# Attention and experts on one core: chunk order, selection matmuls, experts under the last chunk, and a maximum pass that masks in its own instruction

## The reference, cut to what matters

```python
x = x + xattn(layernorm(x), ctx, mask)      # x: 2048 x 256, ctx: 1601 x 256
x = x + ffn(layernorm(x))

def xattn(query, key, mask):                # 16 heads of 16
    scores = (query @ Wq.T) @ (key @ Wk.T).T / 4       # per head
    scores = where(mask == 0 or key index > query index, -inf, scores)
    context = nan_to_num(softmax(scores)) @ (key @ Wv.T)
    return sigmoid(query @ Wg.T + bg) * context @ Wo.T

def ffn(x):                                 # 8 experts, hidden 128, top 2
    scale = softmax(x @ gate_w), all but the two largest set to 0
    xs = scale[e] * x
    return sum over e of (silu(xs @ w1[e]) * (xs @ w3[e])) @ w2[e]
```

## Time and profile before

| what | us |
|---|---|
| median of 3 timed runs | 730.34 (726.5 to 733.89) |
| the profiled execution, own time | 721.41 |
| its span, first to last instruction | 719.7 |
| PE busy | 655.9 (91%) |
| DVE busy | 500.9 (70%) |
| ACT busy | 387.5 (54%) |
| POOL busy | 87.0 (12%) |
| mean granted TensorE clock, share of full speed | 0.925 |

### The profile page before, as it was taken

The page is one execution under the profiler, slowest core; times in us unless marked ns, Lnnn a source line. Parts: engine busy times, 40 slices in busy tenths (PEclk is TensorE's granted clock), DMA queues, the critical chain, the costliest instruction groups (busy, mean ns, idle before and its releaser), DMA issues.

```text
span 719.7 us, 12305 instructions
## 1 busy us (share of the span) xinstructions
PE 655.9 (91%) x4564; PEld 400.3 (56%) x4564; DVE 500.9 (70%) x1043; ACT 387.5 (54%) x778; POOL 87.0 (12%) x167
## 2 busy tenths in 40 slices
PE   5538999969999999999999999999977899999996
PEld 2415756645564554563545455454422587888885
DVE  3112958947868997867898998979630387767764
ACT  1112166545737676555777776657899543332331
POOL 4011233201302011201010102001100000000000
PEclk9767579969988999987999999989999999999999
DMA  9489950710440100750000050000000510616000
GB/s 296 99 144 149 152 64 3 128 22 2 98 51 3 20 3 31 117 178 2 2 3 1 2 118 3 1 1 4 1 2 1 93 27 2 146 25 123 1 30 30
DMA packets 30037, 39.11 MB, mean 54 GB/s; under 512 B 5272, under 2 KB 15896, under 8 KB 29977
## 3 DMA queue, kind: packets, MB, share of 16 engines
q1 hardware_dynamic: 25398, 35.56, 25.7%
q10 hardware_dynamic: 2530, 2.50, 1.1%
q0 software_dynamic: 2048, 0.27, 0.3%
HBM read 27.94 MB, written 9.64 MB: 52 GB/s over the span
## 4 chain that ended last, share of the span: by engine, by line
PE 71%; issue 9%; DMA 9%; DVE 6%; ACT 3%; SPq 1%; POOL 1%; DVEq 0%; ACTq 0%; POOLq 0%
PE bank L1288 15%; PE bank L1268 13%; PE bank L1241 12%; PE bank L1174 8%; DMA k_parts<-stage 4%; PE bank L1349 4%; PE bank L1350 4%; PE bank L1351 4%; DVE pmax L1031 3%; PE bank L1245 3%; DMA q_parts<-stage 2%; PE bank L1367 2%; PE bank L1369 2%; PE bank L1368 2%; DMA qaug<-m_row 2%
## 5 line engine op out<-in xcount | busy, mean ns | idle before, releaser
L1031 DVE TENSOR_REDUCE pmax<-bank 128x1 f32<-128x512 f32 (+4 forms) x640 | 328.4, 575 | 54.8 <-PE bank L1241 36.5
L899 ACT ACTIVATE probs<-bank 128x512 f32<-128x512 f32 (+4 forms) x592 | 281.5, 551 | 128.3 <-PE bank L1268 78.7
L1241 PE MATMUL bank<-kaug,qaug 49*128 49x512 f32 (+4 forms) x640 | 208.3, 441 | 1.6 <-ACT rest L839 1.0
L1268 PE MATMUL bank<-qaug,kaug 51*128 51x512 f32 (+4 forms) x592 | 189.9, 444 | 9.5 <-DMA qaug<-m_row 6.4
L1288 PE MATMUL bank<-probs,vaug 128*32 128x512 f32 (+4 forms) x1184 | 146.3, 580 | 8.8 <-ACT probs L899 8.8
L1268 PEld LDWEIGHTS bank<-qaug,kaug 51*128 51x128 f32 (+1 forms) x592 | 88.1, 190 | 110.7 <-ACT probs L899 58.1
L1241 PEld LDWEIGHTS bank<-kaug,qaug 49*128 49x128 f32 x640 | 106.8, 202 | 34.6 <-DVE pmax L1031 14.7
L1245 PE MATMUL bank<-tri_b,eye_b 64*128 64x128 bf16 (+1 forms) x416 | 60.4, 248 | 0.0
L1288 PEld LDWEIGHTS bank<-probs,vaug 128*32 128x32 f32 (+1 forms) x1184 | 25.6, 111 | 52.2 <-ACT probs L899 31.8
L1349 PE MATMUL bank<-x_hi,w_hi 128*128 128x512 f32 x128 | 51.4, 402 | 0.0
L1350 PE MATMUL bank<-x_lo,w_hi 128*128 128x512 f32 x128 | 50.8, 397 | 0.0
(11 more groups left out here) (104 smaller groups left out, 675.4 us busy)
## 6 DMA issues: line engine op xcount, KB each, us to landing
qaug<-s_dram SPq DMA_DIRECT2D x4, 2048.0 KB, 15.5
qaug<-q_parts SPq DMA_DIRECT2D x24, 256.0 KB, 8.8
kaug<-k_parts SPq DMA_DIRECT2D x18, 256.0 KB, 8.8
q_parts<-stage SPq DMA_DIRECT2D x8, 512.0 KB, 8.2
k_parts<-stage SPq DMA_DIRECT2D x6, 512.0 KB, 13.8
x_sb<-in_x ACTq DMA_DIRECT2D x4, 512.0 KB, 12.0
w_sb<-in_w SPq DMA_DIRECT2D x4, 512.0 KB, 5.4
out<-x_sb SPq DMA_DIRECT2D x4, 512.0 KB, 6.2
```

The lines of the kernel that those rows point to most:

```text
L899: act.activation(probs[0:rows, u % NSLOT, h, off:CH], bank_of(e)[0:rows, off:CH], ACT.Exp, scale=DK ** -0.5).then_inc(act_read, 1)
L1031: dve.tensor_reduce(pmax[:, n % 2, qt, h, slot:slot + 1], bank[:, 0:w], AX_X, ALU.max).then_inc(dve_read, 1)
L1241: last = pe.matmul(bank[:, 0:w], qaug[b:b + ROW_MAX, c % 2, hp, P * qt:P * (qt + 1)], kaug[b:b + ROW_MAX, hp, k0:k0 + w], start=True, stop ...
L1268: last = pe.matmul(bank[0:r, off:CH], kaug[b:b + ROWS, hp, P * j:P * j + r], qaug[b:b + ROWS, c % 2, hp, off:CH], start=True, stop=not dia ...
```

## The change

- Chunks are taken in the order 1, 2, 3, 0 (`ORDER`; `POS` is a chunk's place). Chunk 1 needs keys 0 and 1, so `KEYS_OF` loads both first. Inputs are loaded in another order, some on other queues.
- The first half of the dimensions (`m` = 0: heads 0 to 7) of keys 0 and 1 and of chunk 1's queries doesn't go through DRAM: `sel`, matmuls with a selection matrix of ones, put the parts of two heads at a time where they belong, with mask rows and rows of ones, and ScalarE and VectorE by turns copy the bank to `kaug0`, `kaug1`, `qaug`. The other half takes the trip as before.
- `kaug` is split: `kaug0` for keys 0 to 511, which is all chunk 0 needs, `kaug1` for the rest. `w_hi`, `x_hi` and an expert buffer lie over `kaug1` only. So `ws`, `xs` and the experts of chunk 1 may begin once all scores of chunk 3 are made, beside the attention of chunk 0.
- The maximum pass makes no mask matmuls. VectorE reduces a diagonal piece with `tensor_tensor_reduce`: adds a bf16 tile `causal`, takes the maximum, and writes the sum back to PSUM. `max_pieces` cuts at 512 first and then evenly, as many pieces as before.
- `y` is made turned: six matmuls of 512 columns into two banks, copied by ScalarE (`ycopy`), turned back by TensorE (`yT`), added by VectorE, and written in halves of a chunk. `y` runs two experts behind `a` and `b`, not one.
- GpSimd takes from VectorE the norm (except the first), the parts of weights (`ws`), x's low part, the product `h` and its low part. Scales are loaded per expert. The planner's costs and preferences are new.

The diff, cut to its core:

```diff
+ORDER = (1, 2, 3, 0)
+POS = {c: p for p, c in enumerate(ORDER)}
-Y_BANKS = (0, 1, 2, 7)
+Y_BANKS = (5, 6)
+KEYS_OF = ((0, 1), (2,), (3,), ())
...
+    if p == 0:
+        select = {(w, k): [("sel", w, k, pair) for pair in range(4)] for w, k in (("k", 0), ("k", 1), ("q", c))}
+        return [*norm, ("kq", "k", 0, 0), ("kq", "k", 0, 1), *select["k", 0], *turn, *select["k", 1], ("kq", "q", 0, c),
+                ("kq", "k", 1, 0), *select["q", c], ("kq", "k", 1, 1), ("kload", p), ("kq", "q", 1, c), ("qload", p), *values, *gate]
...
         if kind == "xs":
-            return [("xT1", e[1], 1)] + ([("b", e[1] - 2, E - 1)] if e[1] >= 2 else []) + ([("prologue_end",)] if not e[1] else [])
+            p = POS[e[1]]
+            n = G * (NC - 1) - 1
+            late = [("prologue_end",), ("mred", n)] + all_st(n) if not p else []
+            return [("logits", e[1])] + ([("b", ORDER[p - 2], E - 1)] if p >= 2 else []) + late
...
+        if name == "maxima" and e[1] >= G * (NC - 1):
+            return first_at[e] + 5000
         if name in ("scores", "maxima") and consumer(e) and e[0] != "mT":
-            return free[consumer(e)] - pe_time(e) - DRAIN
+            return free[consumer(e)] - pe_time(e) - DRAIN - (AHEAD if name == "scores" else 0)
...
+            kaug1 = sb("kaug1", [P, HP, KP - CH], F32R, attention)
         w_hi = sb("w_hi", [P, E, 3, D], F32R)
+        x_hi = sb("x_hi", [P, 2, KD, CH], F32R)
+        u_even = sb("u_even", [P, CH], F32)
...
+                elif kind == "ws":
+                    pool.tensor_copy(w_hi[:, ex, :, :], w_sb[:, ex, :, :]).then_inc(w_hi_ready, 1)
+                    pool.wait_ge(w_hi_ready, ex + 1)
+                    pool.tensor_tensor(w_lo[:, ex, :, :], w_sb[:, ex, :, :], w_hi[:, ex, :, :].bitcast(F32), ALU.subtract).then_inc(w_lo_ready, 1)
+                elif kind == "h":
+                    pool.tensor_tensor(v_sb[:, i % 2, :], u_sb[i % 2][:, :], v_sb[:, i % 2, :], ALU.mult).then_inc(h_ready, 1)
+                elif kind == "hl":
+                    pool.tensor_tensor(h_lo[:, i % 2, :], v_sb[:, i % 2, :], h_hi[:, i % 2, :].bitcast(F32), ALU.subtract).then_inc(h_lo_ready, 1)
...
+            for pair in range(4):
+                row, w = 32 * pair, 2 * CH if pair else KEYS
+                dve.tensor_scalar(idle_rows[row:row + 1, 0:w], mask_i[row:row + 1, 0:w], 0, MASKED,
+                                  ALU.is_equal, ALU.mult).then_inc(bias_ready, 1)
...
-                    dve.tensor_reduce(pmax[:, n % 2, qt, h, slot:slot + 1], bank[:, 0:w], AX_X,
-                                      ALU.max).then_inc(dve_read, 1)
+                    if diagonal:
+                        end = CH - P + k0 + w - P * (TPC * ORDER[n // G] + qt)
+                        dve.tensor_tensor_reduce(bank[:, 0:w], bank[:, 0:w], causal[:, end - w:end], 1.0, 2 * MASKED,
+                                                 ALU.add, ALU.max, most).then_inc(dve_read, 1)
+                    else:
+                        dve.tensor_reduce(most, bank[:, 0:w], AX_X, ALU.max).then_inc(dve_read, 1)
...
+                    for part in range(2):
+                        pe.matmul(bank, sel[rows, s + part, :], stage[i % 2][rows, part, :], start=(part == 0), stop=False)
+                    one = slice(32 * pair, 32 * pair + 1)
+                    if what == "k":
+                        pe.matmul(bank, mark[one, 0, :], idle_rows[one, CH * c:CH * (c + 1)], start=False, stop=False)
+                    pe.matmul(bank, mark[one, 1 if what == "k" else 0, :], ones_all[one, :], start=False, stop=True).then_inc(made(e)[0], 1)
...
-                    if diagonal:
-                        for a in range(2):
-                            last = pe.matmul(bank[:, d:w], eye_b[b:b + HALF, a + 1 - side, :],
-                                             tri_b[b:b + HALF, a + 1 - side, 0:w - d], start=False, stop=(a == 1))
...
+                    for a in range(KD):
+                        hi, lo = (w[:, ex, 2, P * a:P * (a + 1)] for w in (w_hi, w_lo))
+                        dst = psum[Y_BANKS[a]][:, :]
+                        pe.matmul(dst, hi, h_hi[:, i % 2, :], start=(ex == 0), stop=False)
+                        pe.matmul(dst, lo, h_hi[:, i % 2, :], start=False, stop=False)
+                        last = pe.matmul(dst, hi, h_lo[:, i % 2, :], start=False, stop=(ex == E - 1))
```

More of the change, by code:

```diff
@@ L237, in make_plan @@
         "values": [[e] for e in values],
-        "weights": [[("xs", 0)]] + [[("ws", ex)] for ex in range(EARLY_WS)],
+        "weights": [[("xs", ORDER[0])]] + [[("ws", ex)] for ex in range(E)],
         "feed": [[e] for e in feed_forward()],
@@ L277, in needs @@
         if kind == "mx":
-            n = e[1]
-            return [("kload", n // G), ("qload", n // G)] + ([("mred", n - 2)] if n >= 2 else [])
+            p, g = e[1] // G, e[1] % G
+            old = [("mred", e[1] - 2)] if e[1] >= 2 else []
+            if p == 0 and g < 2:
+                return [("sel", w, c, pair) for w, c in (("k", 0), ("k", 1), ("q", ORDER[0])) for pair in range(4)] + old
+            return ([("kload", p)] if KEYS_OF[p] else []) + [("qload", p)] + old
         if kind == "mred":
@@ L360, in banks, with serve, on_pool, on_sp @@
     def banks(e):
-        return range(3, 7) if feeding else range(7)
-    def follow(e, at):
-        end = done[e] - LAG.get(e[0], 0)
-        if e[0] in ("stat", "mred", "oT") or e[0] == "kq" and e[3]:
-            others["pool"].append((end, len(plan), e))
-        if e[0] == "kq":
-            end += 1300 if e[3] else 0
-            parts_out.append(end + 3 * HOP)
-        if e[0] == "mT":
-            others["pool"].append((end, len(plan), e))
-        if e[0] in ("kq", "sT", "out"):
-            others["sp"].append((end, len(plan), e))
-        elif e[0] in ("kload", "qload", "sload", "prologue_end"):
-            others["sp"].append((at, len(plan), e))
+        return range(5) if feeding else range(7)
+    def serve(engine, at, cost):
+        free[engine] = max(free[engine], at) + cost
+        return free[engine]
+    def on_pool(e, at):
+        begin = max(free["pool"], at)
+        others["pool"].append((begin, len(plan), e))
+        return serve("pool", at, THEN[e[0]])
+    def on_sp(e, at):
+        others["sp"].append((at, len(plan), e))
+    def alone(e, at):
+        nonlocal loaded
+        kind = e[0]
+        if kind in ALONE:
+            at = serve(ALONE[kind][0], at, ALONE[kind][1]) + 60
+        if kind == "norm" and on_dve(e):
+            return serve("dve", at, 1500) + 60
+        if kind in THEN:
+            at = on_pool(e, at) + 60
+        elif kind in ("kload", "qload"):
+            on_sp(e, at)
+            loaded = max(loaded, at) + LOAD
+            at = loaded + HOP
+        elif kind == "sload":
+            on_sp(e, at)
+            at += PIECE
+        elif kind in ("prologue_end", "out"):
+            on_sp(e, at)
+            at += 10000
+        return at
     def put(e, at):
-        nonlocal last, column, loaded, norm, seen
+        nonlocal last, column, norm, seen, kq_count
         plan.append(e)
@@ L631, in build, with xn_user, sel_dst @@
         block = ctx.enter_context(nc.Block())
+        def xn_user(i):
+            second, c = next(k for k, at in norm_at.items() if at == i)
+            return ("xT1" if second else "xT0", c, 1)
+        def sel_dst(e):
+            _, what, c, pair = e
+            if what == "q":
+                return qaug[:, 0, pair, :]
+            return kaug0[:, pair, :] if c == 0 else kaug1[:, pair, CH * (c - 1):CH * c]
         def lower_part(engine, e):
@@ L714, in _ @@
                     for s in range(2):
[L715 removed]
+                        sp.wait_ge(*parts_left([o for o in kq_list if not fast(o) and kq_at[o] % 2 == s][-1]))
                     for part, name, src in ((0, "w1", w1), (1, "w3", w3)):
```

842 lines of the change are left out of this document (478 added, 364 removed).

## The result

The changed kernel takes 744.37 us (median of 4 runs, 742.75 to 761.08) against 731.11 in the same session: a ratio of 1.024, interval 1.016 to 1.032. A second session gave 744.4 (ratio 1.031, 1.023 to 1.039). Slower by 2.4 to 3%, where 656 us had been forecast, 10% faster. Medians here are over all timed runs, while ratios leave out the runs in a slower state of the chip, so the two need not divide out.

A forecast was written before the change was run, and what follows sets the result against it. DRAM trips were taken to bound the opening, TensorE then VectorE the middle, exponentials the tail, TensorE the experts. 24 + 391 + 43 + 188 = 646 us of span, 656 us as median; own range 630 to 680.

The forecast's parts named there:

- rival 4: Maxima, mostly the middle: the masked maximum takes three passes or more, price 130 us, total 786 us; chance 0.04.
- Opening, 24 forecast: Start to first maximum: half the heads skip the DRAM trip, first maximum at 24 us, not 70.3; bounds 20 to 36.
- Rival 5: Opening: stays near 60 us because something of the other half is wanted first, +30, total 686 us; chance 0.07.
- near 14: Opening: the first norm ends near 14 us instead of 11, after VectorE makes mask rows and a small table.
- Middle, 391 forecast: First maximum to chunk 3's last: 391 us, bounds 361 and 415, with VectorE's work cut from 380.4 to 332 us.
- 332 / 0.85: Middle: 332 us of VectorE work divided by an assumed 85% busy share, giving 391 us.
- Rival 2: Middle: fills better, VectorE 0.92 busy and a tail of 30, total 615 us or so; chance 0.15.
- Rivals 3: Middle: the masked maximum takes a second pass over its columns, 65 us more, total 721 us; chance 0.05.
- Tail, 43 forecast: After chunk 3's last maximum: its scores end 43 us later, by what ScalarE is behind; 52 us before.
- Experts and chunk 0, 188 forecast: Last stretch: experts run beside chunk 0's attention; 176 us of TensorE work plus 12 for start and end.
- rival 1: Last stretch: experts and chunk 0 don't interleave, the chain rules, +33, total 690 us; chance 0.17.
- 25 + 16 + 8: Last stretch, TensorE work besides experts: chunk 0's units 25 us, two routers 16, transposes of o, m and y 8.

The follow-up runs named there:

- e9: N with every maximum a plain one, so keys after a query's own count in the maximum: 716.3 us, ratio 0.987.
- e16: NP with each maximum reducing only the second half of its columns: 702.2 us, ratio 0.968.
- e1: Changed kernel with the mask matmuls back on TensorE and plain maxima on VectorE: 739.7 us.
- e2: Kernel before with only its maximum pass changed to masked maxima: 725.0 us, ratio 0.998.
- N: Changed kernel with all norms on VectorE instead of GpSimd, planner told, so the order shifts: 716.5 us, ratio 0.987.
- e13: Changed kernel with its written order kept, norms computed on VectorE instead of GpSimd: 744.8 us, ratio 1.035.
- e15: N with its written order kept, seven of the eight norms computed on GpSimd: 724.5 us, ratio 0.997.
- e4: Changed kernel with all experts held back until chunk 0's last value matmul: 751.0 us, ratio 1.034.
- e7: N with all experts held back until chunk 0's last value matmul: 723.2 us, ratio 0.996.
- e8: N with the first maxima made to wait until the other half of the heads is back from DRAM: 734.6 us, ratio 1.012.
- NP: N with plain maxima in place of masked ones, so later keys count in the maximum: 716.3 us, ratio 0.987.

## Why the prediction was wrong

The span came out at 742.6 for 646. The four steps miss by 14.6 + 28.9 + 32.5 + 20.6, which is the 96.6 us in full. "Slower" had a chance of 0.04, and rested on rival 4, whose mechanism didn't happen.

*Opening, 24 forecast, 38.6 measured.* The mechanism was right: half of the heads made no trip, and the other half's loads are not in the chain. Rival 5 didn't happen. The step that failed is the norm's end "near 14" and the selections "under the copies". The mask rows end at 11.3 as put, and the statistics are ready at 14.0. But the reciprocal root starts only at 16.1, behind GpSimd's constants (six writes of the selection matrix, four fills and eight masks from 11.78 on), and the norm's first instruction takes 3.13 us, so the norm ends at 21.3: 7.3 us. The low parts of the first key projections stand behind the norm in VectorE's queue (21.22, line 762), so TensorE is idle from 14.1 to 22.1 and the selections of the keys come after the norm, in the chain, for 2 × 2 us. The query projection, put at 2 us, is 3.78, and the other half's key projection holds up its selection by 1.2. That is 14 of the 14.6 us. The bound of 36 was passed.

*Middle, 391 forecast, 420 measured.* The main step that failed is the price of VectorE's time: "332 / 0.85". The work was right, 335 us for 332, and the masked maxima, put at +0.06 us each, cost 0.04 (e9). But taking 48 of 380 us from VectorE was priced as if it set the pace. By that price the 114 us that e16 takes from VectorE in the middle would be 134 us of time; they are 17, as long as ScalarE stays. The lower bound for VectorE's share, 0.80 and 415 us, was passed by 5 us. VectorE at 87% from 240 on in the earlier trace rows was read as the bound; the 68% of ScalarE and the 98% of TensorE beside it belong to the same pace. Rival 2, a fuller middle, was the wrong way round (80%). Rivals 3 and 4, two or three passes of the masked maximum, are ruled out by its 0.59 us. The saving of 17 to 35 us for the mask matmuls of this part was 6 to 11 full-clock us for all of them, less the masked maxima's own cost (e1, e2), and nothing in time.

*Tail, 43 forecast, 75.5 measured.* The step that failed is the number of exponentials left when chunk 3's maxima end. At 2.18 us for four, 43 us are 79 of them; the kernel before had taken 52 us, and a new preference for scores in the plan was to bring part of them forward. ScalarE made 116 in these 75.5 us (58.0 us of work), and 86 in the 53 us of the kernel before (44.1). The 37 more are 20 us at the forecast's rate, and the rest is that rate: 0.65 us each for 0.545 (0.62 before). Chunk 0's maxima, put "for nothing" into the tail, stand in TensorE's queue between the scores (62 matmuls, 17.8 us busy); against the rate of before that can have cost 4 us at most, and no run took them away. Why fewer exponentials were done earlier is the same shared pace as in the middle, argued and not shown. N, in its own order, has 62.6 us for this tail.

*Experts and chunk 0, 188 forecast, 208.6 measured.* TensorE was busy for 192.3 us where 176 had been put, and idle for 16.3 where 12 had. The prediction's own sign for rival 1, silus more than 8 us apart while chunk 0 runs, did appear: they start at 542.8, 559.1, 570.5 and 586.3, and about 5 experts ran beside chunk 0's attention where 14 had been counted. But TensorE was busy for 55.9 of those 60 us (534 to 594), so there it was short of time and not held up by the experts' chain; the sum had too little work in it. Part of rival 1 is in what follows: the chain around the last router's norm, 16 us (605 to 621) in which TensorE worked 11.7. The chain of waits shows the norm:

```profile
614.48 0.72 POOL xn_sb L951
...
615.68 3.63 POOL xn_sb L951 x3
...
619.35 0.67 PE bank L1407 x4
```

"GpSimd gains 4 us per chunk, nobody waits long" was wrong here, by some 3 us (the four instructions take 4.9 us, for 1.6 on VectorE). e13, the same order with its norms on VectorE, takes 206.3 us from the first halves of x to the end, 2.2 less than the 208.5 here, and e15 bounds the cost of all norms at 8. The overlap for which the order was changed is worth only 7 us (e4, e7). Changes of table were not the trouble: ScalarE's timeline has 1.28 us each, and 9 loads beside chunk 0's attention in place of 32 (two more follow for the last router), as the plan keeps exponentials together.

```profile
539.00 1.89 ACT L1107 ACTIVATE probs<-bank 128x256 f32<-128x256 f32 x8 [1.33 <-PE bank L1472]
540.91 1.28 ACT L1140 ACT_TABLE_LOAD   x1
542.75 0.63 ACT L1140 ACTIVATE u_even<-u_even 128x512 f32<-128x512 f32 x1 [0.56 <-DVE u_even L1323]
544.06 1.28 ACT L1107 ACT_TABLE_LOAD   x1 [0.68 <-PE bank L1487]
545.36 1.08 ACT L1107 ACTIVATE probs<-bank 128x512 f32<-128x512 f32 x2
```

The load starts 0.02 us after the activation before it ends (540.89), and the exponential 0.02 after the second load. The Trainium skill, ScalarE: Activation LUTs, What ACT_TABLE_LOAD costs, adds a drain of 1.38 us to each; this trace does not show it, and the measurement decides.

*What the sum left out.* The granted clock was no term of it. 646 us at the clock of before, 0.92, would be 594 full-clock us; the profiled execution needed 742.6 × 0.899 = 668. Those 74 are 80 us of time at 0.92, and the fall of the clock to 0.90 is the other 17. Counted in full-clock us from the stretches, the opening went from 69 × 0.80 = 55 to 38.6 × 0.78 = 30; attention up to the first halves of x from 462 to 442; the rest from 148 to 197. The 49 more at the end are what the prediction had listed there besides experts (25 + 16 + 8); the middle and the tail gave up only 20 for it.

**What stays open.** Why one written order is granted 0.93 and another 0.89, on equal instructions, isn't settled. The drop near 233 and 235 us stands behind a wait of 1.14 us for VectorE in both e13 and the changed kernel, but no run took that wait away, and in N the clock falls at 237.8 us with TensorE busy throughout the ten microseconds before. Orders can't be compared step by step, since every stretch of one differs from the other. With e8 the full-clock us hardly moved (667.3 for 666.2) although it starts 26 us later, so its 18 us cannot be put down to the start alone. N is the best of the versions with every mask in place, 716.5 us, 1.3% faster than the kernel before (interval 0.7 to 2.0%); NP, whose maximum only takes in more keys, is its equal at 716.3. Since N's full-clock us are those of before, its gain is in the clock.

## What to carry to other kernels

When one engine feeds two others from one queue through a few buffers, the busiest reader need not be the bound: price a relief by relieving it alone, then both, before dividing saved work by a fill rate. When an order comes from a planner, an edit that changes one cost changes the whole order: run it once with the old order kept, or the edit gets the blame for its neighbours. And look at span times granted clock beside the time, but never in place of it: e1 has 9 to 11 full-clock us more than its base and is 5 us quicker. Last, before a stretch is priced by the busy share of one engine, count what another engine has left to do when it ends: the tail was 116 exponentials long, whoever was idle in it.

## What the runs showed of the hardware that was not expected

- Span times mean granted clock is constant for a kernel to a standard deviation of 0.7 to 2.5 us within a session, while the spans of the kernel before differ by 18 us in one session. Its runs there differ by their clock, between 0.904 and 0.932, and by little else.
- Orders of the same instructions differ by 28 us in time at equal full-clock us (e13 744.8 and 666.0, N 716.5 and 666.2).
- A masked maximum (two operands, result written back, then an accumulator read shown as 143 ns) takes under 40 ns more of the queue than a plain one, 208 of them 7.7 us. The busy times of its two rows overlap those of their neighbours, and adding them up gave 180 ns.
- An instruction of a norm, 256 columns with two scalars per partition, is 1.22 us on GpSimd and 0.40 on VectorE; but 3.13 on VectorE where it starts beside GpSimd's 3.06 us fill of 3552 columns, in all six traces of the changed kernel and its versions named above.
